# When the Pool queue issues the first batch's loads of head groups 2 and 3 in self-attention

## The chip, the cores and the metric

The kernel runs on one core of one Trainium2 chip. The metric is the device time of one execution in microseconds, lower is better; several executions give a median.

## The reference

The kernel computes one pre-norm decoder layer on x, 4 batches of 1024 tokens with 256 channels: self-attention, cross-attention to 77 context rows, and a mixture of 8 experts of which each takes its 512 best tokens. The change touches self-attention alone:

```
qkv = layernorm(x) @ qkv_w.T + qkv_b          # 16 heads of 16 channels
q, k = apply_rotary(q), apply_rotary(k)
attn = softmax(einsum('bhqd,bhkd->bhqk', q, k) * 0.25)
out = einsum('bhqk,bhkd->bhqd', attn, v)       # then a projection, and x is added
```

## The kernel before

`project_qkv` makes q, k and v for all batches and stores them in DRAM (`qst`, `kst`, `vst`). `attend` then goes through 4 batches. A batch has 4 groups of 4 heads, and each group is done in two halves of 512 queries, so a batch has 8 half groups: `hg` = 0 to 7, group `g = hg // 2`, half `h = hg % 2`. Within a half group, 8 tiles of 128 keys follow each other (`kt`), each in two steps (`u`).

Softmax needs each query's maximum before the exponentials. The kernel makes maxima ahead: for a later half group PE multiplies q and k (L878), DVE reduces each product (L810), a small DVE operation combines them (L816), PE transposes them (`rows`, L884), DVE writes them as two float rows (L823, L825, semaphore `s_ra`), and SP copies these rows into spare partitions of that group's `b_q` tile with 8 small DMAs (L677, semaphore `s_row[h]`). The score products (L929) of a half group contract over these rows too, so that its first score waits for `s_row[h]` (L940). In step `kt == 4` (`LATE`) of half group `hg`, the rows of `hg + 1` are transposed. ACT takes the exponentials of the scores (L748), PE multiplies them with v (L900), and ACT copies the sum out (L735).

The four groups have their own tiles `qs[g]`, `ks[g]`, `vs[g]`. `load_group` fills one: 4 DMAs into q (L483), 4 into k (L483), one into v (L486). Group 0 of the first batch is loaded during the projection. The other loads are issued on Pool. In half group `hg` of group `g`, `hg` even and above 0, Pool waits until the values of group `g - 1` are summed (`s_pv`, L787) and loads that group for the next batch; in the first half group of a batch it loads group 3. PE waits for the load of group `g + 1` in step `kt == 4` of the first half of group `g` (L947).

In the first batch the kernel before loads group 1 behind the first rows of maxima (`s_row[0]` at 128, L773), group 2 directly behind the clearing of pads (L777), and group 3 behind the second rows (`s_row[1]` at 128, L784 and L794).

Each engine's instructions run in the order written. On SP a half group has this order: the sums of the half group before (4 small DMAs, L529, behind `s_oe`); the store of the scaled output of the one before that (L558, behind `s_att`); the rows of maxima of the next half group (L677, behind `s_ra`); the reciprocal sums to DRAM (L540), a wait until they are there (`s_ro`), and 4 DMAs that spread them (L543). On Pool a half group from the third on has: the load, if it has one, then the scaling of an output (L551, behind `s_rb`, the spread reciprocals), which sets `s_att`.

Of the kernel before, what the change touches and what calls it, by code (L numbers as in the profile page):

```python
# [467 lines left out]
def clear_pad(g, pool, a, s, n):  # L468

    for r in range(2):  # L470
        g.memset(a[HR * r + RZ:HR * r + HR, :, :].bitcast(F32), 0.0).then_inc(s, 1)
        pool.wait_ge(s, n + r + 1)


def load_group(sp, q, k, v, s_ld, qst, kst, vst, b, g, part=None):

    for s in range(2):
        if part not in (None, s):
            continue
        heads = slice(G * g + s, G * g + G, 2)  # L480
        for dst, src, runs in ((q, qst, ((0, 0, 16), (16, 0, 32))), (k, kst, ((0, 0, 32), (32, 0, 16)))):
            for to, lo, n in runs:
                sp.dma_start(dst[HR * s + to:HR * s + to + n, :, :].bitcast(F32),  # L483
                             src[b][heads][:, lo:lo + n, :].rearrange("h r n -> r h n")).then_inc(s_ld, 16)
    if part in (None, 2):
        sp.dma_start(v[:].rearrange("p t h d -> p t (h d)"),  # L486
                     vst[b][:, :, G * VS * g:G * VS * g + G * VS]).then_inc(s_ld, 16)
# [92 lines left out]
def attend(nc, ps, ident, group0, s_clear0, stores, ends, tail, firsts, cw, s_cw, x, ost, wts, qst, kst, vst):  # L580
# [5 lines left out]
    with ctx:  # L586
# [29 lines left out]
        s_row = two("b_max_rows_in")  # L616
# [10 lines left out]
        def bodies(eng, body):  # L627
            for i in range(B):
                body(i, i == 0, i == B - 1)
# [126 lines left out]
        @block.gpsimd  # L756
        def _(pool):
            g_ = nc.gpsimd

            def load(b, g):  # L760
                load_group(pool, qs[g], ks[g], vs[g], s_ld[g] if g else s_again, qst, kst, vst, b, g)

            g_.memset(minus[:], -1.0).then_inc(s_minus, 1)
            pool.wait_ge(s_minus, 1)
            end_sums(g_, pool)
            for h in range(2):
                pool.wait_ge(stores[2][h], 16 * (B - 1))
                pool.wait_ge(stores[3][h], 128 * (B - 1))
            for g in range(1, NG):
                clear_pad(g_, pool, qs[g], s_clear[g], 0)  # L770
                clear_pad(g_, pool, ks[g], s_clear[g], 2)
                if g == 2:
                    pool.wait_ge(s_row[0], 128)  # L773
                    load(0, 1)
            g_.memset(rb[:], 1.0).then_inc(s_fill, 1)
            pool.wait_ge(s_fill, 1)
            load(0, 2)  # L777

            def body(i, first, last):
                for hg in range(NH):  # L780
                    g = hg // 2
                    if hg % 2 == 0 and not (last and g > 0):
                        if first and g == 0:
                            pool.wait_ge(s_row[1], 128)  # L784
                        else:

                            pool.wait_ge(s_pv, 8 * (8 * i + hg))  # L787
                        if first and g == 1:
                            for s in stores[2]:
                                pool.wait_ge(s, 16 * B)  # L790
                            for s in stores[3]:
                                pool.wait_ge(s, 128 * B)
                        if g == 0:
                            load(i, 3)  # L794
                        else:
                            load(i + 1, g - 1)
                    if hg > 1 or not first:
                        tail.scale(pool, g_, 8 * i + hg - 2, hg % 2, 4 * i + (hg - 2) // 2 + 1)
            bodies(pool, body)
            tail.scale(pool, g_, NH * B - 2, 0, NG * B)  # L800

# [1301 lines left out]
```

## Time and profile before

| | |
|---|---|
| median of 3 executions | 1182.59 us (1181.22 to 1183.35) |
| profiled execution, its own time | 1181.48 us |
| its span, first to last instruction | 1179.7 us |
| PE busy | 1083.5 us (92%) |
| DVE busy | 1016.5 us (86%) |
| ACT busy | 768.6 us (65%) |
| POOL busy | 352.6 us (30%) |
| mean granted TensorE clock | 0.949 of full speed |

Self-attention runs from about 117 us of the span, where its first products start, to about 786 us; PE and DVE are both busy nine tenths or more in it. A view of the trace names the engine, the line of the kernel, the tiles written and read, and in brackets how long the engine stood idle before and what it waited for. All times are microseconds from the start of the span. In DMA views q0 is the queue that Pool's DMAs go to, q1 that of SP's.

### The profile page before, as it was taken

The page shows a single profiled execution, that of the slowest core. Times are in us where ns is not written, and L with a number is a line of the kernel's source. Part 1 is how long each engine was busy: PE and PEld are TensorE (multiplying, and loading weights), DVE is VectorE, ACT ScalarE, POOL GpSimd, SP SyncE. Part 2 cuts the span into 40 slices and gives each one's busy share as a digit, 9 for nine tenths or more (in the row PEclk, how much of TensorE's full clock was granted, in tenths as well). Part 3 has the DMA queues.
Part 4 walks back from the last instruction along what each step waited for, and adds up shares of the span by engine and source line. Part 5 has one row for each costly group of instructions (what it writes and reads, how often), then busy time and mean ns, then how long its engine had stood idle before and what let it go on. Part 6 is the DMA issues. An engine that isn't in the chain of part 4 may idle for free. (4 is left out here: it accounts for less than half of the span.)

```text
span 1179.7 us, 22856 instructions
## 1 busy us (share of the span) xinstructions
PE 1083.5 (92%) x8540; PEld 595.9 (51%) x8540; DVE 1016.5 (86%) x2168; ACT 768.6 (65%) x932; POOL 352.6 (30%) x316
## 2 busy tenths in 40 slices
PE   7899999999999999999999999998984059999998
PEld 6775333333333333333333333347773048888897
DVE  8999889999999999999999999716998985766663
ACT  4551378888888888888887888863565014555653
POOL 2657812202220221122022000022100023765675
PEclk9997699999999999999999999999997559999999
DMA  7787664504422441343044100036532022554443
GB/s 240 252 267 232 148 101 98 96 18 78 75 57 39 81 77 31 65 79 70 22 84 75 21 12 17 17 103 214 178 108 95 0 72 65 152 146 122 111 112 36
DMA packets 84681, 113.95 MB, mean 97 GB/s; under 512 B 25056, under 2 KB 57568, under 8 KB 84576
## 3 DMA queue, kind: packets, MB, share of 16 engines
q1 hardware_dynamic: 66256, 69.82, 20.0%
q0 software_dynamic: 15024, 36.17, 17.2%
q10 hardware_dynamic: 3296, 6.56, 1.5%
q8 instruction: 65, 1.06, 0.4%
q14 instruction: 40, 0.33, 0.1%
HBM read 73.31 MB, written 38.27 MB: 95 GB/s over the span
## 5 line engine op out<-in xcount | busy, mean ns | idle before, releaser
L810 DVE TENSOR_REDUCE b_max_halves<-banks 128x1 f32<-128x512 f32 x1024 | 626.7, 680 | 14.3 <-PE banks L878 14.2
L748 ACT ACTIVATE b_probs<-banks 128x1024 f32<-128x1024 f32 x512 | 520.7, 1027 | 146.4 <-PE banks L929 146.4
L878 PE MATMUL banks<-b_k,b_q 62*128 62x512 f32 x1024 | 398.7, 470 | 6.7 <-DVE b_max_halves L810 1.8
L929 PE MATMUL banks<-b_q,b_k 64*128 64x512 f32 x1024 | 385.8, 456 | 3.8 <-DMA b_q<-b_max_rows 3.5
L900 PE MATMUL banks<-b_probs,b_v 128*17 128x256 f32 (+1 forms) x3840 | 315.5, 401 | 0.2 <-ACT b_probs L748 0.2
L929 PEld LDWEIGHTS banks<-b_q,b_k 64*128 64x128 f32 x1024 | 156.9, 186 | 224.2 <-issue 167.8
L878 PEld LDWEIGHTS banks<-b_k,b_q 62*128 62x128 f32 x1024 | 162.0, 190 | 41.6 <-DVE b_max_halves L810 39.3
L900 PEld LDWEIGHTS banks<-b_probs,b_v 128*17 128x17 f32 x3840 | 63.9, 95 | 165.6 <-issue 95.9
L551 POOL TENSOR_TENSOR b_att<-b_out,b_rec_spread 128x512 f32<-128x512 f32 x32 | 41.1, 1284 | 311.5 <-DMA b_rec_spread<-reciprocals 311.2
L483 POOL DMA_DIRECT2D b_q<-q_stacks x60 | 31.8, 533 | 227.8 <-PE banks L900 215.6
L1849 DVE TENSOR_TENSOR e_hTl<-e_hT,e_hTh 128x512 fp32r<-128x512 f32 x64 | 47.6, 745 | 48.3 <-ACT e_hT L1603 48.3
L1629 POOL DMA_INDIRECT e_x<-rows,d_idx x32 | 45.3, 1416 | 110.2 <-DVE d_wx L1804 56.7
L1600 ACT ACTIVATE e_hTh<-banks,e_b 128x512 fp32r<-128x512 f32 x64 | 44.1, 690 | 51.9 <-PE banks L1961 48.3
L1961 PE MATMUL banks<-e_w2h,e_hTh 128*128 128x256 f32 x256 | 73.1, 286 | 0.0
L1961 PE MATMUL banks<-e_w2l,e_hTh 128*128 128x256 f32 x256 | 72.4, 283 | 0.0
L1961 PE MATMUL banks<-e_w2h,e_hTl 128*128 128x256 f32 x256 | 72.4, 283 | 0.0
L1586 ACT ACTIVATE e_xTh<-banks 128x512 fp32r<-128x512 f32 x16 | 8.7, 596 | 83.1 <-PE banks L1949 83.1
L1652 POOL DMA_INDIRECT out_x<-c_x,d_idx x32 | 55.3, 1728 | 17.7 <-DVE c_x L1882 11.0
L1961 PE MATMUL banks<-e_xTh,e_w1h 128*128 128x512 f32 x128 | 53.6, 419 | 3.2 <-DVE e_xTl L1817 2.6
L1961 PE MATMUL banks<-e_xTl,e_w1h 128*128 128x512 f32 x128 | 50.9, 398 | 0.0
L1961 PE MATMUL banks<-e_xTh,e_w1l 128*128 128x512 f32 x128 | 50.6, 396 | 0.0
L392 POOL TENSOR_TENSOR a_rotated<-a_by_even,a_by_odd 128x1024 f32<-128x1024 f32 x13 | 36.4, 2800 | 45.6 <-DVE a_by_odd L331 45.2
(259 smaller groups left out, 1477.9 us busy)
## 6 DMA issues: line engine op xcount, KB each, us to landing
e_w<-in_w SPq DMA_DIRECT2D x16, 1024.0 KB
q_stacks<-a_parts SPq DMA_DIRECT2D x32, 256.0 KB, 4.0
k_stacks<-a_parts SPq DMA_DIRECT2D x32, 256.0 KB, 4.1
b_q<-q_stacks POOLq DMA_DIRECT2D x30, 256.0 KB, 5.3
b_k<-k_stacks POOLq DMA_DIRECT2D x30, 256.0 KB, 6.4
v_tiles<-a_v ACTq DMA_DIRECT2D x8, 544.0 KB, 3.7
b_rec_spread<-reciprocals SPq DMA_DIRECT2D x128, 32.0 KB, 1.8
attended<-b_att SPq DMA_DIRECT2D x128, 32.0 KB, 2.7
```

Source lines behind the costliest of these rows:

```text
L392: g.tensor_tensor(to, by_even[:, q], by_odd[:, q], ALU.add).then_inc(s_eo, 1)
L551: g.tensor_tensor(self.att[:, x, :], self.osb[:, x, :], self.rb[:, x, :], ALU.mult).then_inc(self.s_att, 1)
L748: nc.scalar.activation(pr[:, S % NP, u], ps[:, 2 * u:2 * u + 2, :], ACT.Exp, scale=D ** -0.5).then_inc(s_ex[u], 1)
L810: v.tensor_reduce(mxp[:, (k // NB) % 2, s, p, t, kh:kh + 1], ps[:, bank(last), :], AX.X, ALU.max)\
L878: nc.tensor.matmul(ps[:, bank(last), :], qs[g][stack, p, at:at + P], ks[g][stack, p, CH * kh:CH * kh + CH], start=True, stop=True).then_in ...
L900: last = nc.tensor.matmul(ps[VW * j:VW * j + VS, PV, at], vs[hg // 2][:, kt, j, :], pr[:, S % NP, j // 2, j % 2, at], start=(kt == 0), sto ...
L929: return nc.tensor.matmul(ps[:, 2 * u + s, :], ks[g][stack, u, P * kt:P * kt + P], qs[g][stack, u, CH * h:CH * h + CH], start=True, stop=True)
L1600: nc.scalar.activation(hh[:, f, :], ps[:, UP[f % len(UP)], :], ACT.Gelu, bias=b1[:, x, f:f + 1])
L1629: g.indirect_dma_start(xe[:, x, h, :], None, xrow, bass.IndirectOffsetOnAxis(ap=idx[:, n, h:h + 1], axis=0))\
L1652: g.indirect_dma_start(out, bass.IndirectOffsetOnAxis(ap=idx[:, n, h:h + 1], axis=0), y[:, h, :], None, compute_op=ALU.add).then_inc(s_sc, 16)
L1849: v.tensor_tensor(hl[:, f, :], hf[:, f % NH, :], hh[:, f, :], ALU.subtract).then_inc(s_hl, 1)
L1961: ins = mm(o, a, b, start=(start and m == 0), stop=(stop and m == len(pairs) - 1))
```

## The change

In the first batch, the load of group 2 is issued behind the wait for the second rows of maxima (those of half group 1), where the load of group 3 was. The load of group 3 is issued in half group 1, behind a new wait for the third rows (those of half group 2, `s_row[0]` at 256). Later batches are unchanged.

```
             g_.memset(rb[:], 1.0).then_inc(s_fill, 1)
             pool.wait_ge(s_fill, 1)
-            load(0, 2)
...
                         if first and g == 0:
                             pool.wait_ge(s_row[1], 128)
+                            load(0, 2)
...
-                        if g == 0:
+                        if g == 0 and not first:
                             load(i, 3)
-                        else:
+                        elif g:
                             load(i + 1, g - 1)
+                    if first and hg == 1:
+                        pool.wait_ge(s_row[0], 256)
+                        load(0, 3)
                     if hg > 1 or not first:
                         tail.scale(pool, g_, 8 * i + hg - 2, hg % 2, 4 * i + (hg - 2) // 2 + 1)
```

## Rows read from the trace of the kernel before

**Rows 1.** Waits: engine, line, waited for: total us, times, longest; 132 to 182 us.

```profile
PE banks L929 <- DMA b_q<-b_max_rows: 2.7, 1, 2.7
```

**Rows 2.** Waits of PE alone, 182 to 420 us.

```profile
PE banks L878 <- DVE b_max_halves L810: 0.2, 1, 0.2
```

**Rows 3.** Timeline of PE: start, us, engine, line, operation, tiles, count [idle before].

```profile
146.37 0.33 PE L884 MATMUL banks<-ident,b_max 128*128 128x128 f32 x1
...
156.95 0.49 PE L929 MATMUL banks<-b_q,b_k 64*128 64x512 f32 x1 [2.69 <-DMA b_q<-b_max_rows]
...
157.63 1.05 PE L900 MATMUL banks<-b_probs,b_v 128*17 128x256 f32 x8
...
170.90 0.33 PE L884 MATMUL banks<-ident,b_max 128*128 128x128 f32 x1
...
178.70 0.50 PE L929 MATMUL banks<-b_q,b_k 64*128 64x512 f32 x1
...
199.00 0.50 PE L929 MATMUL banks<-b_q,b_k 64*128 64x512 f32 x1
...
219.50 0.50 PE L929 MATMUL banks<-b_q,b_k 64*128 64x512 f32 x1
```

**Rows 4.** Timeline of SP's queue: start, us of issuing, line, tiles, count.

```profile
147.64 4.97 SPq L677 DMA_DIRECT2D b_q<-b_max_rows  x8
...
172.09 5.00 SPq L677 DMA_DIRECT2D b_q<-b_max_rows  x8
179.51 0.36 SPq L540 DMA_DIRECT2D reciprocals<-b_rec  x1
180.99 1.71 SPq L543 DMA_DIRECT2D b_rec_spread<-reciprocals  x4
183.47 2.46 SPq L529 DMA_DIRECT2D b_sums<-b_out  x4
189.07 1.70 SPq L558 DMA_DIRECT2D attended<-b_att  x4
192.37 5.03 SPq L677 DMA_DIRECT2D b_q<-b_max_rows  x8
...
213.39 5.02 SPq L677 DMA_DIRECT2D b_q<-b_max_rows  x8
```

**Rows 5.** Timeline of POOL: the loads' first and last issues, and one scaling.

```profile
142.44 1.04 POOL L483 DMA_DIRECT2D b_q<-q_stacks  x2 [0.29 <-POOL b_rec_spread L775]
...
146.51 0.92 POOL L486 DMA_DIRECT2D b_v<-v_tiles  x1
157.19 1.04 POOL L483 DMA_DIRECT2D b_q<-q_stacks  x2 [9.76 <-DMA b_q<-b_max_rows]
...
182.75 1.04 POOL L483 DMA_DIRECT2D b_q<-q_stacks  x2 [20.58 <-PE banks L900]
...
187.74 1.30 POOL L551 TENSOR_TENSOR b_att<-b_out,b_rec_spread 128x512 f32<-128x512 f32 x1
```

**Rows 6.** Windows: busy us of PE, PEld, DVE, ACT, POOL, then PEclk, DMA share, GB/s.

```profile
154.00:155.00 1.00, 0.26 (x8) 0.00 (x0) 0.81 (x2) 0.80 (x1) 0.00 (x0) 1.00 0.22 42
...
158.00:159.00 1.00, 1.00 (x10) 0.39 (x4) 0.78 (x2) 0.77 (x1) 1.00 (x3) 0.50 0.76 160
...
158.00:161.00 3.00, 3.00 (x22) 0.91 (x16) 2.06 (x4) 1.79 (x2) 3.00 (x7) 0.51 0.91 191
```

**Rows 7.** DMA view, all packets, 147.7 to 153.9 us (they are all q0's).

```profile
DMA packets 301, 0.98 MB, mean 158 GB/s; under 512 B 66, under 2 KB 66, under 8 KB 301
...
q0 software_dynamic: 301, 0.98, 101.6%
```

**Rows 8.** DMA view by queue, packets, MB, share of 16 engines: 158.4 to 169.2 us.

```profile
q0 software_dynamic: 591, 1.85, 98.2%
```

**Rows 9.** DMA view by queue, 184.0 to 194.8 us.

```profile
q0 software_dynamic: 589, 1.84, 97.4%
q1 hardware_dynamic: 260, 0.09, 5.6%
```

More of the change, by code:

```diff
@@ L776, in _ @@
             pool.wait_ge(s_fill, 1)
-            load(0, 2)
             def body(i, first, last):
@@ L784, in body @@
                             pool.wait_ge(s_row[1], 128)
+                            load(0, 2)
                         else:
@@ L792, in body @@
                                 pool.wait_ge(s, 128 * B)
-                        if g == 0:
+                        if g == 0 and not first:
                             load(i, 3)
-                        else:
+                        elif g:
                             load(i + 1, g - 1)
+                    if first and hg == 1:
+                        pool.wait_ge(s_row[0], 256)
+                        load(0, 3)
                     if hg > 1 or not first:
```

## The prediction

> **What bounds the kernel now.** I read the busy table first: PE is busy 92% of the span and DVE 86%, so a change that only moves DMAs can gain only where PE stands still. The waits say where that is in self-attention: from 132 to 182 us PE waits once for the rows of maxima, 2.7 us [rows 1]; from 182 to 420 us it waits 0.2 us in all, for DVE [rows 2]. PE's timeline places the wait: the first score of half group 1 starts at 156.95, 2.69 us late [rows 3]. I call the first scores of half groups 1, 2, 3, 4 S1 to S4: 156.95, 178.70, 199.00, 219.50 [rows 3].
>
> Where S1 should be: without a wait S2 follows its transposition of maxima by 178.70 - 170.90 = 7.80 us. The one before S1 is at 146.37, so S1 was due at 154.17 [rows 3]. From S2 to S3 is 20.30 us, from S1 to S2 21.75: 1.45 more. The reason is in the granted clock: 0.51 from 158 to 161 us [rows 6], the lower of the two levels (1.2 GHz), right after PE had stood still; eight value products take 1.05 us there [rows 3]. So the stall costs 2.78 + 1.45 = 4.23 us.
>
> Why the rows are late: SP issues their 8 DMAs from 147.64 to 152.61 [rows 4]. Pool issued group 2's load from 142.44 to 147.43 [rows 5]. From 147.7 to 153.9 every packet moved is q0's, 301 of them, at 101.6% of the 16 DMA engines [rows 7]; none is of the rows, though the first of their DMAs was issued 6 us earlier and the last by 152.61. The engines empty in the microsecond from 154 (share 0.22) [rows 6], and PE starts at 156.95. So in this trace a small DMA issued behind a whole load is served when that load is through.
>
> **What the change removes.** Group 2's load leaves this place. Its nine issues took 5 us of Pool [rows 5], which Pool now waits away; nothing stands behind them but the wait for the second rows. The rows of half group 1 then meet no load. How soon do they land? For S4, SP's issue is late (213.39 + 5.02 = 218.41) and S4 follows at 219.50, 1.09 us later [rows 3, 4]. By that they land at 152.61 + 1.09 = 153.70, before 154.17. S1 = 154.17, the clock stays, and S2 = 154.17 + 20.30 = 174.47: -4.23 us. Bounds: gain 4.23 at most; at least 2.5, if the rows came 0.3 late and the clock fell anyway.
>
> **What it moves.** Group 2's load starts as group 3's did, at once behind the second rows: at about 154.2 rather than 157.19. It needs 10.8 us in the engines (98.2% of that stretch is q0's, 1.85 MB [rows 8]), from about 155.4 to 166.2, while its user, step kt 4 of half group 2, comes some 10 us behind S2, at 184. Covered by 18 us. The rows for half group 2, at 172.09 - 4.23 = 167.9 on SP, come after it. No cost.
>
> **What it adds.** Group 3's load now waits for these third rows: issued 167.9 to 172.9, landed 1.09 later at 174.0; Pool starts 0.24 later (as 157.19 behind 156.95 [rows 3, 5]), at 174.2, and is done issuing at 179.2. Its user is a whole group away (kt 4 of half group 4, past 220): covered. But behind it on Pool stands the reload of group 0 for batch 1, which went out at 182.75, 4.05 behind S2 [rows 3, 5]; it is due at 178.5 and is issued at 179.2 to 184.2, with no gap. Two loads now stand in one queue. The first packets come 1.1 to 1.3 us behind the first issue (157.19, and a share of 0.76 in the microsecond from 158 [rows 5, 6]); with 1.25 they come at 175.45. Each load takes 0.982 x 10.8 = 10.6 us of all engines [rows 8], two take 21.2; what q1 has ahead of the rows I put at 1.0 us (0.6 in the stretch of [rows 9], and the 128 KB store). So the engines are full until about 197.7.
>
> The rows of half group 3 are due on SP at 192.37 - 4.23 = 188.1, and S3 at 194.77. Before, the load that ran beside them went out 9.6 us ahead of them, and by 182.75 + 1.25 + 10.8 its packets were through at 194.8, 4 us ahead of S3, so it cost nothing [rows 3, 4, 5]. Now the backlog ends 2.9 us behind the due time of S3. From first packet (142.44 + 1.25 = 143.7 [rows 5]) to PE's restart the old stall took 156.95 - 143.7 = 13.25 us for a load of 10.6: 2.65 more. The same here gives 175.45 + 21.2 + 1.0 + 2.65 = 200.3; with the quick landing of 1.09 it is 197.7 + 1.1 = 198.8. I take 199.9, nearer the old stall, which is the same situation. S3 is then 5.1 us late, and the clock dip comes again: 1.45 us at the one price seen, up to 2.9 if the longer stall brings two, 0.5 at least.
>
> SP's order adds a second route to the same place. The reciprocals go out at 179.51 - 4.23 = 175.3 [rows 4], just behind group 3's first two DMAs (Pool issues one per 0.52 us). They are held about 1 us, so the spread's 4 DMAs are issued at 178.1 to 179.8, behind nearly all of group 3's load, and land near 187. Pool's scaling, which waits for them, goes from 184.2 (free) to 187.1 to 188.4; SP's store behind it ends at 190.2; the rows are issued at 190.2 to 195.2 rather than from 188.1. That is still ahead of the end of the backlog, so it adds nothing to 199.9.
>
> **Sum.** S3 = 199.9 against 199.00, +0.9; S4 = 199.9 + 20.30 + 1.45 = 221.65 against 219.50, +2.15 (the 0.2 us that SP's lateness cost at S4 is gained, as SP has sent its spread sooner relative to S3). Everything behind S4 moves along. On the profiled execution's own time 1181.48 that is 1183.6; on the median 1182.59, 1.1 above it, 1184.7. Own range: S3 at 198.8 with half a microsecond of dip, +0.1, to S3 at 200.3 with two dips, +4.0: 1182.7 to 1186.6.
>
> The Trainium skill speaks against my order of service: "DMA: Bandwidth & Descriptors", section "Queues, rings and completion order", has each DMA engine alternate between the queues it has work for, a packet of descriptors from one before it switches. By that rule a row of maxima would wait for one packet, not for the load, which is rival 1 below. The stretch with 301 packets of q0 and none of q1 does not look so [rows 7].
>
> **Rivals.**
> (1) The small DMAs get through between the loads' packets. For: during the load from 184.0 to 194.8, 260 packets of q1 were served [rows 9], sums issued at 183.47 to 185.93 among them [rows 4]. Against: those were issued while the load was still being issued, so service in the order of issue explains them too, and in [rows 7] DMAs issued behind the whole load stood. If so, S3 is at 194.77 and S4 at 215.07, -4.4 us: 1178.2. This is the one on the other side. It decides from the point where the rows of half group 3 land before 194.8. Chance 0.22.
> (2) The backlog costs, but less: rows served by engines that finish early, landing at 196.8, stall 2.0, one dip. -4.23 + 2.0 + 1.45 - 0.2 = -1.0: 1181.6. For: the engines don't all end together. Against: one late engine of 16 holds the count. Chance 0.14.
> (3) SP's chain becomes the bound: the reciprocals are held behind four or more of the load's DMAs, the spread falls into the reload of group 0, lands at 191 or later, and rows are issued at 195 to 200: S3 at 201.1, +4 with the dip: 1186.6; if the spread falls behind the whole reload, it lands at 198.7, the rows end at 207 and it is +11. For: the three events (landing, Pool's start, 175.3) lie within 1.5 us. Against: only two DMAs are ahead by the times above. Chance 0.14.
> The forecast has 0.50.
>
> **How the numbers follow.** 0.2%, what a measurement here can tell from no change, is 2.4 us: 1180.2 and 1185.0. Faster: rival 1, 0.22, and a little of rival 2: 0.23. Slower: rival 3, 0.14, and somewhat under half of the forecast's own range, 0.23: 0.37. The same: the rest of the forecast and of rival 2, 0.40. The range reaches down to rival 1 and up over the nearer end of rival 3: 1178.0 to 1187.0; outside are rival 3's far end and what I have not thought of.
>
> **What would show it.** S1 near 154.2 with no wait and no clock dip behind it; S2 near 174.5. Group 3's load on Pool at 174 to 179 and the next load right behind. The spread landing near 187, the scaling at 187 rather than 184. PE idle some 5 us ahead of S3, with the rows of maxima named, and the clock at its lower level behind it. If q1 has packets between 190 and 197, while q0 is full, the order of service is wrong and rival 1 holds. If S1 still waits, the load was not the reason, and the gain is gone as well.

## The result, and the profile after

The changed kernel takes 1186.44 us (median of nine executions, 1184.00 to 1188.25) against 1182.79 us for the kernel before (ten executions, measured together): ratio 1.0029, 95% interval 1.0020 to 1.0038. It is slower, by 3.4 us by the ratio and 3.7 by the medians. A tenth execution of it took 1612 us at a granted clock of 0.551 and is left out. The forecast was 1184.7, with 1178.0 to 1187.0 as its range.

The profiled execution took 1188.25 us (span 1186.5), the slowest of the nine, against 1181.48. That difference of 6.8 us is not all the change's: its first transposition of maxima in the loop comes at 149.29 against 146.37 before [rows 3], 2.9 us later. That is not the change's: PE's first transpositions of the span are already 1.5 us later (13.05 against 11.54), and in seven other kernels whose program is the changed one's up to there this transposition comes between 145.98 and 147.53. So stretches are compared, not times of the span.

PE's timeline (start, us, engine, line, operation, idle before) shows where it waits now. Line numbers behind L800 are 3 higher than before.

```profile
149.29 0.33 PE L887 MATMUL banks<-ident,b_max 128*128 128x128 f32 x1
...
157.12 0.49 PE L932 MATMUL banks<-b_q,b_k 64*128 64x512 f32 x1
...
177.44 0.50 PE L932 MATMUL banks<-b_q,b_k 64*128 64x512 f32 x1
...
189.91 0.33 PE L887 MATMUL banks<-ident,b_max 128*128 128x128 f32 x1
...
203.84 0.79 PE L932 MATMUL banks<-b_q,b_k 64*128 64x512 f32 x1 [6.04 <-DMA b_q<-b_max_rows]
...
204.99 1.05 PE L903 MATMUL banks<-b_probs,b_v 128*17 128x256 f32 x8
...
226.26 0.50 PE L932 MATMUL banks<-b_q,b_k 64*128 64x512 f32 x1
...
287.18 0.50 PE L932 MATMUL banks<-b_q,b_k 64*128 64x512 f32 x1
```

S1 to S4 are at 157.12, 177.44, 203.84 and 226.26, and S7 at 287.18. S1 follows the transposition by 7.83 us, without a wait; it took 10.58 before [rows 3]. S1 to S2 takes 20.32 (21.75 before), S2 to S3 26.40 (20.30), S3 to S4 22.42 (20.50). So the first wait is gone with its clock dip, 4.18 us, and a wait of 6.04 us stands at S3, with a larger dip behind it. From the first transposition to S7 it is 137.89 us; before, S7 is at 280.42, 134.05 behind. The loss is 3.84 us. Behind S7 the two agree: from 290 to 780 us PE waits for rows once in each, 0.9 us, and up to the end of the span the loss is 3.9.

SP's queue (start, us of issuing), to set against [rows 4]:

```profile
170.80 5.01 SPq L677 DMA_DIRECT2D b_q<-b_max_rows  x8
178.24 0.36 SPq L540 DMA_DIRECT2D reciprocals<-b_rec  x1
182.84 1.94 SPq L543 DMA_DIRECT2D b_rec_spread<-reciprocals  x4
184.82 2.47 SPq L529 DMA_DIRECT2D b_sums<-b_out  x4
194.97 2.70 SPq L558 DMA_DIRECT2D attended<-b_att  x4
197.72 5.03 SPq L677 DMA_DIRECT2D b_q<-b_max_rows  x8
```

And Pool's, to set against [rows 5]:

```profile
157.12 1.04 POOL L483 DMA_DIRECT2D b_q<-q_stacks  x2 [12.50 <-DMA b_q<-b_max_rows]
...
177.16 1.04 POOL L483 DMA_DIRECT2D b_q<-q_stacks  x2 [15.06 <-DMA b_q<-b_max_rows]
...
182.12 1.04 POOL L483 DMA_DIRECT2D b_q<-q_stacks  x2
...
193.67 1.27 POOL L551 TENSOR_TENSOR b_att<-b_out,b_rec_spread 128x512 f32<-128x512 f32 x1 [6.59 <-DMA b_rec_spread<-reciprocals]
```

The reader is to see one chain. Group 3's load starts at 177.16. SP issues the reciprocals at 178.24, and waits until 182.84 before it can spread them; before, 179.51 and 180.99 [rows 4]. Pool issues the reload of group 0 from 182.12, so that the spread stands between two loads. Its DMAs take 9.2 us to land, as the DMA view of 178 to 184.8 us says in its last column (us to landing):

```profile
b_rec_spread<-reciprocals SPq DMA_DIRECT2D x4, 32.0 KB, 9.2
reciprocals<-b_rec SPq DMA_DIRECT2D x1, 8.0 KB, 4.6
```

Pool idles 6.59 us for it, scales at 193.67 (16.2 us behind S2; 9.0 before [rows 3, 5]), SP's store follows at 194.97, and only then do the rows of maxima leave, from 197.72 to 202.75. They were due at S2 + 13.7 = 191.1. S3 comes at 203.84: 1.09 us behind the last issue, the quick landing of the prediction. The DMA engines had emptied before that. Windows (busy PE, PEld, DVE, ACT, POOL, then PEclk, DMA share, GB/s) show the end of the backlog in the microsecond from 200, and the low clock behind the wait:

```profile
199.00:200.00 1.00, 0.00 (x0) 0.00 (x0) 0.25 (x1) 0.00 (x0) 0.00 (x0) 1.00 0.86 169
200.00:201.00 1.00, 0.00 (x0) 0.00 (x0) 0.00 (x0) 0.00 (x0) 0.00 (x0) 1.00 0.55 138
201.00:202.00 1.00, 0.00 (x0) 0.00 (x0) 0.00 (x0) 0.00 (x0) 0.00 (x0) 0.99 0.02 4
204.00:208.00 4.00, 4.00 (x24) 1.14 (x24) 2.48 (x4) 1.76 (x2) 0.48 (x1) 0.50 0.24 63
```

So SP's chain set S3 in this execution, not the backlog. Would the backlog alone have made it late too? The first experiment asks that.

### The profile page after: what moved, and what is told of

It reads as the page before. It is cut to its first block and busy times, and to the rows that moved or that the text cites. A ratio compares the mean times of both kernels' runs of the same rounds, so it can differ in the third digit from the quotient of the medians.

```text
span 1186.5 us, 22857 instructions
## 1 busy us (share of the span) xinstructions
PE 1083.6 (91%) x8540; PEld 596.4 (50%) x8540; DVE 1015.2 (86%) x2168; ACT 767.8 (65%) x932; POOL 352.3 (30%) x316
## 5 line engine op out<-in xcount | busy, mean ns | idle before, releaser
L1655 POOL DMA_INDIRECT out_x<-c_x,d_idx x32 | 55.3, 1728 | 17.7 <-DVE c_x L1885 11.0
```

What stands on the lines that cost most here:

```text
L1655: g.indirect_dma_start(out, bass.IndirectOffsetOnAxis(ap=idx[:, n, h:h + 1], axis=0), y[:, h, :], None, compute_op=ALU.add).then_inc(s_sc, 16)
```

## The experiments

All edits but one are on the changed kernel, and none changes what the kernel computes. The four of each batch ran on one chip with the kernel before.

**SP sends the rows ahead of the store.**

```
+                    early = first and hg == 2
+                    if early:
+                        sp.wait_ge(s_ra, n["rows"] + hg + 1)
+                        rows(sp, (hg + 1) // 2 % NG, (hg + 1) % 2)
                     if hg > 1:
                         tail.store(sp, m - 1, i, (hg - 2) // 2, 1 - x)
...
-                    if not (last and hg == NH - 1):
+                    if not (last and hg == NH - 1) and not early:
```

> The changed kernel, with SP issuing the rows of maxima of half group 3 ahead of the store it had before them, in the first batch. In the changed kernel S3 (the first score of half group 3) is 6.0 us late, and its rows left SP at 197.7 to 202.8 rather than from 190.9. Theory A, both things hold: SP's chain (reciprocals, spread, scaling, store) sets the last 2 us, and the backlog of two loads, which leaves the engines at 200.2, would hold the rows by itself. Then the rows are issued on time, nothing of them is served while the loads run, S3 is about 4 us late, and the time is 2 us under the changed kernel's, near 1184.8. Rival B, SP's chain alone is the cause: S3 is on time, 1178.5 to 1179. Rival C, the backlog alone is the cause and the chain does not matter: S3 6 us late as before, 1186.8.

Measured: 1185.34 us, ratio to before 1.0017 (0.9994 to 1.0039). PE's wait at S3, and SP's issue of the rows:

```profile
198.93 0.79 PE L936 MATMUL banks<-b_q,b_k 64*128 64x512 f32 x1 [4.41 <-DMA b_q<-b_max_rows]
```

```profile
187.82 5.01 SPq L677 DMA_DIRECT2D b_q<-b_max_rows  x8
```

The rows leave SP at 13.7 us behind S2 (174.14), as due, and S3 is still 4.41 us late. From 192.9, when all 8 have been issued, to 196.0 the DMA view has 171 packets of q0 and none of q1:

```profile
DMA packets 172, 0.54 MB, mean 174 GB/s; under 512 B 45, under 2 KB 45, under 8 KB 171
...
q0 software_dynamic: 171, 0.52, 101.3%
q8 instruction: 1, 0.02, 2.8%
```

Theory A holds: with the rows sent on time the backlog alone makes S3 4.4 us late, and with SP's chain ahead of them they leave so late that it is 6.0. (The chain is not free of the backlog: its spread waits among the loads' DMAs. What the chain does beside a single load is the third experiment.) B and C fall by the profile (4.41 is neither 0 nor 6). The times exclude B, but not C: the interval of the ratio is 5.3 us wide and reaches up to 1187.3.

**Both loads behind the second rows**, where no spread and no store stand in the way.

```
                             pool.wait_ge(s_row[1], 128)
                             load(0, 2)
+                            load(0, 3)
...
-                    if first and hg == 1:
-                        pool.wait_ge(s_row[0], 256)
-                        load(0, 3)
```

> Groups 2 and 3 are both loaded behind the second rows of maxima, one directly behind the other, in half group 1, where no scaling and no store stands ahead of the next rows on SP. Theory A: the engines are full for 21.2 us from S1 + 1.3, rows of half group 2 (due to leave SP at S1 + 13.7) are served after that, S2 comes at S1 + 24 to 25.4 instead of + 20.3, the clock drops behind it (1.5 to 2.1 us), S3 is on time: +1 to +3 us against the kernel before, 1183.8 to 1185.8. Rival B, SP's chain alone: no stall at S2, 1178.5. Rival D, small DMAs get through between the loads' packets: the same, and q1 has packets of the rows while q0 is full.

Measured: 1185.25 us, ratio 1.0024 (1.0014 to 1.0035). The rows left SP on time, at 167.74 to 172.74, and from 173.0 to 175.3 all packets are q0's:

```profile
179.48 0.79 PE L930 MATMUL banks<-b_q,b_k 64*128 64x512 f32 x1 [5.03 <-DMA b_q<-b_max_rows]
```

```profile
DMA packets 127, 0.39 MB, mean 171 GB/s; under 512 B 31, under 2 KB 31, under 8 KB 127
...
q0 software_dynamic: 127, 0.39, 100.3%
```

S2 comes at S1 + 25.4 (theory A: 24 to 25.4). So two loads without a gap between them cost 4.4 to 5.0 us in both places where the next rows fell behind them. B and D fall.

**Only the reload is held back**: group 3's load stays where the change put it, the reload of group 0 goes behind the fourth rows.

```
+                    if first and hg == 3:
+                        pool.wait_ge(s_row[1], 256)
+                        load(1, 0)
...
-                        elif g:
+                        elif g and not (first and g == 1):
                             load(i + 1, g - 1)
```

> The changed kernel, with the reload of group 0 for batch 1 held back to half group 3, behind the fourth rows of maxima. Group 3's load stays behind the third rows. Theory A: the load of group 3 costs nothing where it is; it was the pair without a gap. S1, S2, S3 come without a wait, no clock dip: 4.2 us under the kernel before. The reload (10.6 us of the engines) now shares them with the weights of the next stage, which SP issues in half group 3 (about 5.5 us of the engines), full until about S3 + 18, so S4 is 0 to 1 us late: 1178.4 to 1179.8. Rival E: the reciprocals' and the spread's delay behind group 3's load alone is enough to make the rows late: S3 still 1 to 3 us late, 1181 to 1184.

Measured: 1184.99 us, ratio 1.0018 (1.0009 to 1.0027). Theory A's prediction failed, and the rival was right. PE's timeline has two waits:

```profile
197.65 0.50 PE L935 MATMUL banks<-b_q,b_k 64*128 64x512 f32 x1 [2.45 <-DMA b_q<-b_max_rows]
...
221.56 0.50 PE L935 MATMUL banks<-b_q,b_k 64*128 64x512 f32 x1 [2.17 <-DMA b_q<-b_max_rows]
```

For the first wait, SP and Pool:

```profile
179.33 1.71 SPq L543 DMA_DIRECT2D b_rec_spread<-reciprocals  x4
...
188.49 1.28 POOL L551 TENSOR_TENSOR b_att<-b_out,b_rec_spread 128x512 f32<-128x512 f32 x1 [8.93 <-DMA b_rec_spread<-reciprocals]
...
189.80 1.70 SPq L558 DMA_DIRECT2D attended<-b_att  x4
191.54 5.03 SPq L677 DMA_DIRECT2D b_q<-b_max_rows  x8
```

The spread leaves at 179.33 and Pool's scaling has to wait until 188.49; SP's store goes out at 189.80 and the rows from 191.54 to 196.57, 1.08 us ahead of S3. One load alone, put where the reciprocals are due, is enough. The place behind the third rows is wrong in itself.

The second wait is the reload's, in its new place beside the weights of the next stage: the rows leave SP at 215.46, S3 + 17.8, and S4 follows the last issue by 1.08. What holds SP there is its sums, whose four small DMAs take 8.32 us to issue, against 2.46 in the kernel before; why one of them takes 5.41 us the profile doesn't say.

**Group 3's load in half group 3, behind the fourth rows**; the reload where it was before.

```
-                    if first and hg == 1:
-                        pool.wait_ge(s_row[0], 256)
+                    if first and hg == 3:
+                        pool.wait_ge(s_row[1], 256)
                         load(0, 3)
```

> Group 2's load behind the second rows, as in the changed kernel; group 3's load in half group 3, behind the fourth rows of maxima; the reload of group 0 for batch 1 goes out in half group 2 as in the kernel before. Theory A: no two loads stand in the queue, S1 to S3 without a wait, the spread and the scaling as early as in the kernel before; S4 0 to 1 us late, because group 3's load and the next stage's weights share the engines: 1178.4 to 1179.8. Rival F: moving group 2's load is not what removes the wait at S1 or the gain is not there when repeated: within 1 us of 1182.8.

Measured: 1185.31 us, ratio 1.0022 (1.0012 to 1.0032). S1 to S3 come without a wait, 20.30 and 20.28 us apart, so the first half of the change does gain what it should (rival F falls); but S4 is 5.04 us late, not 0 to 1:

```profile
196.75 0.34 SPq L540 DMA_DIRECT2D reciprocals<-b_rec  x1
202.17 2.73 SPq L543 DMA_DIRECT2D b_rec_spread<-reciprocals  x4
...
215.27 5.02 SPq L677 DMA_DIRECT2D b_q<-b_max_rows  x8
```

The load starts at 195.68, the reciprocals at 196.75: the same collision one half group later. SP waits for them, then issues the weights of the next stage (in its program for `hg == 2`, so in half group 3 by PE's count), and the rows leave at S3 + 19.3 instead of + 13.7; S4 follows the last issue by 1.09.

The next batch takes this apart: the weights away, the collision away, both away.

**Only the weights moved**, on the kernel before (`first and hg == 4` for `hg == 2` at L717), so that they leave SP two half groups later, in half group 5 by PE's count.

> The kernel before, with nothing changed but the load of the next stage's weights, which SP issues behind the spread of half group 4 instead of half group 2. Both theories: S4's 0.2 us goes and may come back two half groups later; 1182.7, no difference. It is the control for the runs that move these weights.

Measured: 1184.10 us against 1183.24, ratio 1.0008 (0.9999 to 1.0017). No clear difference; a wait of 0.78 us appears at S6 in its place.

**The weights moved, group 3's load still behind the fourth rows.**

> Group 3's load in half group 3 behind the fourth rows of maxima, as in the run before it, and the weights moved to half group 4. There S4 was 5.0 us late, and its rows left SP late because SP had waited 5.4 us for the reciprocals behind the load, then issued the weights. Theory A, SP's order sets S4: the spread leaves SP at S3 + 6.2 and lands when the load is through, at about S3 + 12; scaling, store, and rows end at S3 + 19.7; S4 is 0.3 to 0.6 us late and the time is 4 us under the kernel before, 1178.7 to 1179.5. Rival B, it was the amount: the weights' 5.5 us of the engines behind the load's 10.6; also on time. They differ in where the rows leave SP: A has them late by some 1 us, B when due (S3 + 13.6). Rival G: gains at S1 don't reach the end: 1182 or more.

Measured: 1183.15 us, ratio 1.0000 (0.9991 to 1.0008). SP and PE:

```profile
199.74 1.70 SPq L543 DMA_DIRECT2D b_rec_spread<-reciprocals  x4
201.48 2.46 SPq L529 DMA_DIRECT2D b_sums<-b_out  x4
211.25 1.70 SPq L558 DMA_DIRECT2D attended<-b_att  x4
212.99 5.03 SPq L677 DMA_DIRECT2D b_q<-b_max_rows  x8
```

```profile
219.12 0.79 PE L932 MATMUL banks<-b_q,b_k 64*128 64x512 f32 x1 [3.42 <-DMA b_q<-b_max_rows]
```

The rows leave late (S3 + 17.7), and S4 follows the last issue by 1.10, so SP's order it is, as A says; but A's size was wrong, 3.42 us against 0.3 to 0.6. I had the scaling at once behind the load's end; Pool scales at 209.95, 14.6 us behind S3.

**Group 3's load behind the scaling of half group 3**, the weights where they were.

```
-                    if first and hg == 1:
-                        pool.wait_ge(s_row[0], 256)
-                        load(0, 3)
                     if hg > 1 or not first:
                         tail.scale(pool, g_, 8 * i + hg - 2, hg % 2, 4 * i + (hg - 2) // 2 + 1)
+                    if first and hg == 3:
+                        load(0, 3)
```

> Group 3's load in half group 3, but behind the scaling there, so behind the reciprocals and the spread; the weights where they were. Theory A: the reciprocals come back at once (1.5 us), the spread lands by S3 + 4, the load goes out at S3 + 5.5 beside SP's weights; together 16 us of the engines, full until S3 + 21, so the rows of half group 4, issued by S3 + 19.5, are served behind them: S4 1.5 to 3 us late and a clock dip of 0 to 2 us. 1180 to 1182.5. Rival B, only SP's order counts: S4 on time, 1178.5.

Measured: 1183.81 us, ratio 1.0003 (0.9993 to 1.0013). The reciprocals come back in 1.5 us, but S4 is 4.82 us late, more than A's 1.5 to 3. The rows leave SP by 215.21, only 1.7 us later than due; the DMA engines are busy until about 217 (share 0.83 in the microsecond from 216, 0.17 in the next), and S4 comes at 219.93. So most of it is the backlog of load and weights by itself. (For this kernel and the one before it the profiled execution loses 2.5 us up to S7 against the kernel before, while the ratios show 0 to 0.4. The profiled execution of the kernel before took 1181.48, 1.8 us under that kernel's median here, which may be most of it; with one profile of each this stays open.)

**Both**: the load behind the scaling, the weights moved.

> The same with the weights moved to half group 4. Theory A: nothing meets anything, as for every other load of the kernel (each goes out about 4 us behind its half group's start): no wait for rows of maxima in the first batch, no clock dip in it. 4.2 to 4.4 us under the kernel before: 1178.3. Rival G: the time is within 1 us of the kernel before, which would show that PE's saved wait is given back elsewhere.

Measured: 1179.64 us against 1183.24, ratio 0.9968 (0.9957 to 0.9979). It is the only kernel here faster than the one before, by 3.6 to 3.8 us. All that PE waits for from 130 to 500 us:

```profile
PE banks L880 <- DVE b_max_halves L812: 0.9, 3, 0.6
PE banks L931 <- DMA b_q<-b_max_rows: 0.5, 1, 0.5
```

Pool's load goes out at 202.21, 6.7 us behind S3 (195.55), and SP's chain and the rows (209.20, S3 + 13.65) pass in time:

```profile
196.35 0.34 SPq L540 DMA_DIRECT2D reciprocals<-b_rec  x1
197.82 1.70 SPq L543 DMA_DIRECT2D b_rec_spread<-reciprocals  x4
200.31 3.15 SPq L529 DMA_DIRECT2D b_sums<-b_out  x4
203.50 1.97 SPq L558 DMA_DIRECT2D attended<-b_att  x4
209.20 5.03 SPq L677 DMA_DIRECT2D b_q<-b_max_rows  x8
```

From the first transposition in the loop (147.12) to S7 (277.44) it is 130.32 us, 3.73 under the kernel before. The 4.2 us that the change set out to gain are real; the 0.5 us wait, at S6, is the moved weights'.

| kernel | ratio to before | waits for rows | first transposition to S7, against before |
|---|---|---|---|
| changed | 1.0029 | S3 6.04 | +3.84 |
| rows ahead of store | 1.0017 | S3 4.41 | +2.44 |
| both behind second rows | 1.0024 | S2 5.03 | +2.48 |
| reload held | 1.0018 | S3 2.45, S4 2.17 | +3.07 |
| fourth rows | 1.0022 | S4 5.04 | +3.30 |
| kernel before, weights moved | 1.0008 | S1 2.56, S6 0.78 | +0.59 |
| fourth rows, weights | 1.0000 | S4 3.42, S6 0.66 | +2.51 |
| behind scaling | 1.0003 | S4 4.82 | +2.51 |
| behind scaling, weights | 0.9968 | S6 0.49 | -3.73 |

## Why the prediction was right, and where it was not

**The wait removed: right.** S2 came 28.15 us behind the first transposition, against 32.33 [rows 3]: 4.18 us gained, 4.23 forecast. No wait, no dip.

**A wait put in at S3 by two loads without a gap: right, as a mechanism.** It was forecast 5.1 us late; the backlog by itself makes it 4.41, and 5.03 where it was put at S2. The packets of q1 stay away while q0 is full in both windows shown, as the prediction read it in [rows 7]. Rival 1, small DMAs between the loads' packets, is refuted for DMAs issued behind a whole load, and with it what the rule of the Trainium skill, "DMA: Bandwidth & Descriptors", section "Queues, rings and completion order", would have made of this case. The prediction's sign for rival 1, packets of q1 between 190 and 197 while q0 is full, did appear in the changed kernel: 146 from 190 to 193 and 151 from 193 to 197, with q0 at 82.5% and 97.9%. But none is of the rows, which left SP only from 197.72. SP had issued the spread and the sums from 182.84 to 187.29, while Pool was issuing the reload (182.12 to 187.08), so these packets fit service in the order of issue as well.

**SP's chain adds nothing: wrong.** This is the step that failed. The prediction had the reciprocals held for about 1 us, because only two of the load's DMAs were ahead of them. Two were (a third was issued beside them), but they carry 128 and 256 KB; at the 1.85 MB in 10.8 us of [rows 8] that is an estimated 2.3 us of the engines, 3.8 with the third, and the reciprocals took 4.6 to land where they had taken 1.5 [rows 4]. So the hold was mis-sized: 3.1 us, not 1. The spread therefore left at S2 + 5.4 instead of + 3.6, beside the first DMAs of the reload, and landed in 9.2 us; scaling at S2 + 16.2 instead of + 12.6, rows at S2 + 20.3 instead of + 15.7. With that the chain passed the backlog and S3 was 6.04 us late, 0.9 more than forecast. This is the nearer end of rival 3, held at 0.14 and priced at 1186.6; the time was 1186.44. (Its price is high for its own terms: S3 at 201.1 with the one dip of 1.45 is +3.35; +4 needs a dip of 2.1, which is what came.) The experiment that took the store out of the rows' way gives back 1.6 us of the wait. That the time is still inside the range is in part luck: the route put at nothing set S3, and it happened to pass the backlog by only 1.6 us.

**The dip: mis-sized.** 1.45 us was forecast at the one price seen, with up to 2.9 as the bound; S3 to S4 took 22.42, so 2.1 over 20.3.

**What passes unseen.** The prediction doesn't name the weights that SP loads in half group 3. In the changed kernel they were harmless (S4 had no wait). Beside a load in that half group they are not: behind the scaling, S4 is 4.82 us late with them and has no wait without; behind the fourth rows, taking them away leaves 3.42 of 5.04.

**The sum.** -4.18 + 6.04 + 2.1 is +4.0; with the 0.2 us gained at S4 it is 3.8, the 3.84 of the traces and the 3.4 to 3.7 of the times. The forecast of +2.15 had the sign, and was 1.7 us short: 0.9 by SP's chain, 0.7 by the dip.

## What to carry to other kernels

A bulk load is not free because the engines have idle time on average: look up when each small DMA that somebody waits for is due, and place the load so that all of its bytes are through before, or its first byte comes after. A gate on an event at the start of a period puts the load just ahead of everything that the period sends first; here one load there delayed a round trip of 8 KB, 1.5 us long, by 2.1 to 3.9 us (five kernels) and, through a queue that runs in order, the rows it had been moved out of the way of. Moving a transfer away from one collision has to be followed to the next transfer behind it on the same queue, since two loads without a gap are one load of twice the length.

## What the runs showed of the hardware

The dip behind a wait went with how long PE stood still. With 2.2 to 2.7 us of waiting, the following half group took 21.7 to 21.8 us (four cases: 21.69, 21.74 without the wait that ends it, 21.78, 21.75), 1.4 over 20.3. With 3.4 to 6.0 us it took 22.1 to 23.0 (22.97, 22.69, 22.42, 22.11, 22.90, 22.42), 1.8 to 2.7 over, with no order by length inside the group. Three waits of 0.49 to 0.78 us, at S6, have no dip behind them (20.31, 20.33, 20.33). The granted clock says the same: it stayed at 1.00 over the 2.6 to 2.8 us behind the three short waits, was 0.61 to 0.74 over the first 2.3 to 2.5 us behind the four middle ones, and 0.50, the lower level, for at least 3 us behind the six long ones.

A small DMA issued among the DMAs of a load landed, in the changed kernel, in its place in the order of issue. These are the first three DMAs of group 3's load and the reciprocals (KB each, us to landing), issued between 177.16 and 178.3:

```profile
b_q<-q_stacks POOLq DMA_DIRECT2D x1, 256.0 KB, 3.8
b_k<-k_stacks POOLq DMA_DIRECT2D x1, 256.0 KB, 5.1
b_q<-q_stacks POOLq DMA_DIRECT2D x1, 128.0 KB, 3.2
reciprocals<-b_rec SPq DMA_DIRECT2D x1, 8.0 KB, 4.6
```

The 128 KB went first, from 177.16. The next of the load, issued at 177.7, landed at 181.5; the reciprocals, issued at 178.24, at 182.84; the third, issued at 178.2, at 183.3. Of the 144 packets of q1 up to 182.9, 125 were moved between 179.4 and 180.5 and the last 3 only behind 180.9, so a few late packets set when SP goes on. In five kernels whose load starts 1.1 us ahead of the reciprocals these took 3.6, 3.6, 3.7, 4.6 and 5.4 us, so the same place does not give the same delay.
